# Two-layer graph network on one core: pairs of adjacency columns as one f16 stationary element, and node blocks interleaved by four

## The reference

```
def L0(X, adj, W, b):                       # W is 128x64
    deg = clip(sum(adj, 1) + 1, 1)
    h_neigh = (adj @ X + X) / deg
    out = relu(concat([X, h_neigh], 1) @ W + b)
    return out / max(norm(out), 1e-12)
def L1(F, adj, W):                          # W is 64x128
    neigh = adj @ F / (sum(adj, 1) + 1)
    return concat([F, neigh], -1) @ W.T
x = layernorm(x + L0(x, adj, W0, b0))
x = layernorm(x + L1(x, adj, W1))
```

## Time and profile before

| | us |
|---|---|
| runs, median of 3 (lowest, highest) | 773.65 (772.61, 775.78) |
| the profiled execution's own time | 773.52 |
| its span | 771.7 |
| PE busy / weight loads busy | 671.0 / 621.8 |
| DVE busy | 690.4 |
| ACT busy | 611.3 |
| POOL busy | 297.1 |
| adjacency and other transfers | 274.8 MB, 356 GB/s over the span |

### The profile page before, as it was taken

The page is one execution under the profiler, slowest core; times in us unless marked ns, Lnnn a source line. Parts: engine busy times, 40 slices in busy tenths (PEclk is TensorE's granted clock), DMA queues, the critical chain, the costliest instruction groups (busy, mean ns, idle before and its releaser), DMA issues.

```text
span 771.7 us, 31938 instructions
## 1 busy us (share of the span) xinstructions
PE 671.0 (87%) x13173; PEld 621.8 (81%) x13173; DVE 690.4 (89%) x2662; ACT 611.3 (79%) x815; POOL 297.1 (39%) x302
## 2 busy tenths in 40 slices
PE   1457787978789888999999999999999999998994
PEld 0346677868688787888899999999999999998994
DVE  4699988989999999999899999899998989888884
ACT  4879898999999898989898988787878979750032
POOL 2235523533233323365534525253444425231034
PEclk9978897989999999999999999999999999999997
DMA  9999999999999999999999999999999999900004
GB/s 301 385 420 420 417 417 420 420 419 419 420 417 420 399 419 407 412 417 405 418 407 419 407 419 401 390 375 403 386 406 379 395 384 383 393 5 3 3 18 99
DMA packets 46139, 274.79 MB, mean 356 GB/s; under 512 B 12646, under 2 KB 12710, under 8 KB 13222
## 3 DMA queue, kind: packets, MB, share of 16 engines
q1 hardware_dynamic: 45184, 270.55, 87.2%
q0 software_dynamic: 576, 2.10, 0.8%
q10 hardware_dynamic: 230, 0.07, 0.0%
HBM read 270.60 MB, written 2.10 MB: 353 GB/s over the span
## 4 chain that ended last, share of the span: by engine, by line
PE 48%; DVE 18%; issue 11%; DMA 11%; ACT 8%; POOL 3%; ACTq 0%; DVEq 0%; SPq 0%; POOLq 0%
PE s_ps L372 26%; PE u_ps L391 8%; DMA a_in<-in_adj 8%; PE p_ps L358 6%; ACT junk L570 6%; DVE t_sb L783 4%; DVE e L776 4%; DMA xl<-in_x 3%; PE z_ps L438 2%; POOL small L1158 2%; PE p_ps L450 1%; PE z_ps L423 1%; DVE a_in L783 1%; DVE q_sb L848 1%; DVE y_sb L842 1%
## 5 line engine op out<-in xcount | busy, mean ns | idle before, releaser
L570 ACT ACTIVATE junk<-a_in 128x2048 uint8<-128x2048 uint16 x256 | 489.7, 1920 | 3.8 <-DMA a_in<-in_adj 3.7
L372 PE MATMUL s_ps<-xh,t_sb 128*128 128x129 f16 x4096 | 381.8, 248 | 21.6 <-DVE t_sb L783 19.0
L372 PEld LDWEIGHTS s_ps<-xh,t_sb 128*128 128x128 fp8e4 x4096 | 308.0, 101 | 50.2 <-DVE t_sb L783 22.7
L776 DVE TENSOR_SCALAR e<-a_in 128x2048 fp8e4<-128x2048 f32 x256 | 310.9, 1223 | 11.1 <-DMA a_in<-in_adj 10.4
L1166 POOL COPY store<-pk 128x32 uint32<-128x32 uint32 (+1 forms) x250 | 215.0, 901 | 229.7 <-ACT pk L579 229.7
L358 PE MATMUL p_ps<-pow_bf,e 128*128 128x16 bf16 x4096 | 142.0, 170 | 54.1 <-DVE e L776 49.6
L358 PEld LDWEIGHTS p_ps<-pow_bf,e 128*128 128x128 fp8e4 x4096 | 128.7, 97 | 67.2 <-DVE e L776 60.1
L783 DVE TENSOR_SCALAR t_sb<-pk 128x128 uint32<-128x128 uint32 x1024 | 151.2, 221 | 6.7 <-ACT pk L579 5.6
L1158 POOL TENSOR_TENSOR small<-small,minus_half 128x4 f32<-128x4 f32 x32 | 67.8, 2117 | 199.7 <-DVE small L836 149.1
L391 PE MATMUL u_ps<-xh,u_sb 128*128 128x64 f16 x2976 | 105.0, 192 | 0.0
L391 PEld LDWEIGHTS u_ps<-xh,u_sb 128*128 128x128 fp8e4 x2976 | 99.8, 97 | 1.2
(11 more groups left out here) (119 smaller groups left out, 463.0 us busy)
## 6 DMA issues: line engine op xcount, KB each, us to landing
a_in<-in_adj SPq DMA_DIRECT2D x256, 1024.0 KB, 10.6
xl<-in_x POOLq DMA_DIRECT2D x4, 512.0 KB, 15.8
out_h<-e SPq DMA_DIRECT2D x8, 256.0 KB, 2.7
b_sb<-in_L_gnn_b ACTq DMA_DIRECT2D x3, 0.2 KB
w_sb<-in_L_gnn_W ACTq DMA_DIRECT2D x1, 32.0 KB
w_raw<-in_L_gnn_W ACTq DMA_DIRECT2D x1, 32.0 KB
```

The costliest lines, as they stand in the source:

```text
L372: last = nc.tensor.matmul(s_ps[:, n % 2, at:GW], t_sb[:, b, :], xh[:, b, at:GW], start=(b == 0), stop=False)
L570: nc.scalar.activation(junk[:, t % 2, :], halves[t % R], ACT.Copy, scale=1.0 / 128, accum_out=half_sum[:, n, c:c + 1]).then_inc(s_half, 1)
L776: nc.vector.tensor_scalar(e8[:, c, :], a_in[:, t % R, :], 1.0, None, ALU.is_equal, saturate=False).then_inc(s_e, 1)
```

## The change

Nodes are renumbered inside the kernel: four row blocks take 512 nodes, and block 4j + r holds the nodes 512j + 4p + r for p = 0 to 127. A transfer of `adj` therefore takes every fourth row, in runs of 8 KB as before. Four neighbouring columns now belong to four column blocks. The code of an entry is a byte, 60 or 61, and two neighbouring bytes read as one f16 are (1084 + a + 256 b) / 1024, with a and b the two entries. One product packs both blocks: 32 packing products per row block, each with a stationary operand of 128 f16 that lie 4 bytes apart. ACT subtracts the constant part and writes 16-bit results (256 per half). After unpacking, the two blocks of a pair are interleaved byte by byte, so every stationary operand of the sums, the catch-up and the tail has a step of 2 bytes. x and the output move in runs of 1 KB, x by ACT's queue in place of POOL's. x and `acc` no longer lie side by side; a tile `cat_in` takes the copy of x that POOL makes (`own_rows`) and the mean.

```diff
+IL = 4
+CODE = 60
+CODE_SUM = 255.0 * (1024 + CODE)
-        e8 = sb("e8", [P, NC, CH], FP8)
+        e8 = sb("e8", [P, NC, CH], U8)
-        t_sb = sb("t_sb", [P, NB, P], FP8)
+        t_sb = sb("t_sb", [P, NB // 2, 2 * P], FP8)
-        u_sb = sb("u_sb", [P, PIECE * W, P], FP8)
+        u_sb = sb("u_sb", [P, PIECE * W // 2, 2 * P], FP8)
-        xl = sb("xl", [P, NB, 2 * F], F32)
+        xl = sb("xl", [P, 2, NB, F], F32)
+        cat_in = sb("cat_in", [P, BR, 2 * F], F32)
-        x_in = xl[:, :, 0:F]
-        acc = xl[:, :, F:2 * F]
+        x_in, acc = xl[:, 0, :, :], xl[:, 1, :, :]
+        e_pair = e8[:, :, :].rearrange("p c i -> p (c i)").bitcast(F16).rearrange(
+            "p (c j i h) -> p c j i h", c=NC, i=P, h=IL // 2)
+        out_j = out.rearrange("(j p r) f -> p j (r f)", p=P, r=IL)
+        x_j = x.rearrange("(j p r) f -> p j (r f)", p=P, r=IL)
+        adj_j = adj.rearrange("(j p r) c -> j r p c", p=P, r=IL)
...
-                    sp.dma_start(a_in[:, t % R, :], adj_v[n, :, c * CH:(c + 1) * CH]).then_inc(s_in[t % R], 16)
+                    sp.dma_start(a_in[:, t % R, :], adj_j[n // IL, n % IL, :, c * CH:(c + 1) * CH]).then_inc(s_in[t % R], 16)
...
-                for b in range(CB):
-                    at = ((c % 2) * CB + b) * PK
-                    last = nc.tensor.matmul(p_ps[:, c // 2, at:at + PK], e8[:, c, b * P:(b + 1) * P],
-                                            pow_bf[:, :], start=True, stop=True)
+                for u in range(CB // 2):
+                    at = ((c % 2) * CB // 2 + u) * PK
+                    last = nc.tensor.matmul(p_ps[:, c // 2, at:at + PK], e_pair[:, c, u // 2, :, u % 2],
+                                            pow_h[:, :], start=True, stop=True)
...
-                    last = nc.tensor.matmul(s_ps[:, n % 2, at:GW], t_sb[:, b, :], xh[:, b, at:GW],
+                    last = nc.tensor.matmul(s_ps[:, n % 2, at:GW], t_sb[:, b // 2, b % 2::2], xh[:, b, at:GW],
...
-                            last = nc.tensor.matmul(u_rows[:, r, 0:F], u_sb[:, r * W + b, :],
+                            last = nc.tensor.matmul(u_rows[:, r, 0:F], u_sb[:, (r * W + b) // 2, b % 2::2],
...
+                pe.wait_ge(s_own, e + 1)
...
-                    last = nc.tensor.transpose(c_ps[:, k, :], xl[:, e * BR + k, :], ident[:, :])
+                    last = nc.tensor.transpose(c_ps[:, k, :], cat_in[:, k, :], ident[:, :])
...
+            for q in range(NC):
+                act.dma_start(x_in[:, q * CB:(q + 1) * CB, :].rearrange("p (j r) f -> p j (r f)", r=IL),
+                              x_j[:, q * CB // IL:(q + 1) * CB // IL, :]).then_inc(s_x[q], 16)
...
-                nc.scalar.copy(pk[:, n % 2, h * 512:(h + 1) * 512], p_ps[:, h, :]).then_inc(s_pk, 1)
+                nc.scalar.activation(pk_u[:, n % 2, h * 256:(h + 1) * 256], p_ps[:, h, 0:256], ACT.Copy,
+                                     bias=-CODE_SUM, scale=1024.0).then_inc(s_pk, 1)
...
-                nc.vector.tensor_scalar(e8[:, c, :], a_in[:, t % R, :], 1.0, None, ALU.is_equal,
-                                        saturate=False).then_inc(s_e, 1)
+                nc.vector.tensor_scalar(e8[:, c, :], a_in[:, t % R, :], 1.0, float(CODE), ALU.is_equal,
+                                        ALU.add).then_inc(s_e, 1)
...
-                nc.vector.tensor_tensor(acc[:, rows, :], s_sb[:, :, :], bc(small[:, 0, :], BR),
+                if e:
+                    dve.wait_ge(s_catps, e)
+                nc.vector.tensor_tensor(cat_in[:, :, F:2 * F], s_sb[:, :, :], bc(small[:, 0, :], BR),
                                         ALU.mult).then_inc(s_mean, 1)
...
-            for q in range(NC):
-                pool.dma_start(x_in[:, q * CB:(q + 1) * CB, :], x_v[:, q * CB:(q + 1) * CB, :]).then_inc(s_x[q], 16)
+            def own_rows(e):
+
+                if e:
+                    pool.wait_ge(s_catps, e)
+                else:
+                    for q in range(NC):
+                        pool.wait_ge(s_x[q], 16)
+                nc.gpsimd.tensor_copy(cat_in[:, :, 0:F], x_in[:, e * BR:(e + 1) * BR, :]).then_inc(s_own, 1)
...
                 if n:
                     keep(n - 1)
+                if e >= 0 and k == 0:
+                    own_rows(e)
```

More of the change, by code:

```diff
@@ L154, in gnn_kernel @@
         pow_f = sb("pow_f", [P, PK], F32)
-        pow_bf = sb("pow_bf", [P, PK], BF16)
+        pow_h = sb("pow_h", [P, PK], F16)
         ones_f = sb("ones_f", [P, P], F32)
@@ L213, in gnn_kernel @@
         s_mean = sem("s_mean")
+        s_own = sem("s_own")
         s_catps = sem("s_catps")
@@ L240, in gnn_kernel @@
         s_pool = sem("s_pool")
-        out_g = out.rearrange("(g k p) f -> g p k f", k=TG, p=P)
+        out_j = out.rearrange("(j p r) f -> p j (r f)", p=P, r=IL)
+        x_j = x.rearrange("(j p r) f -> p j (r f)", p=P, r=IL)
+        adj_j = adj.rearrange("(j p r) c -> j r p c", p=P, r=IL)
         out_v = out.rearrange("(e k p) f -> e p k f", k=BR, p=P)
@@ L247, in words @@
         def words(ap):
-            return ap.rearrange("p b i -> p (b i)").bitcast(U32).rearrange("p (b w) -> p b w", w=P // 4)
+            return ap.rearrange("p u i -> p (u i)").bitcast(U32).rearrange("p (u w) -> p u w", w=P // 2)
         pk_w = pk[:, :, :].rearrange("p s i -> p (s i)").bitcast(U32).rearrange("p (s w) -> p s w", s=2)
@@ L327, in _ @@
                     sp.wait_ge(s_o_dve, g - NA + 1)
-                sp.dma_start(out_g[g, :, :, :], o_sb[:, g % 4, :, :]).then_inc(s_out[g % 4], 16)
+                sp.dma_start(out_j[:, g * TG // IL:(g + 1) * TG // IL, :],
+                             o_sb[:, g % 4, :, :].rearrange("p (j r) f -> p j (r f)", r=IL)).then_inc(s_out[g % 4], 16)
             for i in range(4):
@@ L449, in tail_sums @@
                         if j < NV:
-                            last = nc.tensor.matmul(v_ps[j % 3][:, r, :], v_sb[:, j % VR, r * W + b, :],
+                            last = nc.tensor.matmul(v_ps[j % 3][:, r, :], v_sb[:, j % VR, (r * W + b) // 2, b % 2::2],
                                                     xh[:, at + b, 0:HP], start=(b == 0), stop=(b == W - 1))
@@ L453, in tail_sums @@
                         for part in range(2):
-                            last = nc.tensor.matmul(v_ps[j % 3][:, r, 0:F], v_sb[:, j % VR, r * W + b, :],
+                            last = nc.tensor.matmul(v_ps[j % 3][:, r, 0:F], v_sb[:, j % VR, (r * W + b) // 2, b % 2::2],
                                                     xh[:, at + b, part * F:(part + 1) * F],
@@ L718, in _ @@
             nc.vector.tensor_scalar(id8[:, :], ident[:, :], 2.0, None, ALU.mult, saturate=False)
-            nc.vector.tensor_copy(pow_bf[:, :], pow_f[:, :]).then_inc(s_pow, 1)
+            nc.vector.tensor_copy(pow_h[:, :], pow_f[:, :]).then_inc(s_pow, 1)
             link(nc.vector.memset(xh[:, :, 2 * HP:GW], XS))
@@ L790, in unpack @@
                     dve.wait_ge(s_sum, (n - 1) * 2 + h + 1)
-                half = slice(h * NB // 2, (h + 1) * NB // 2)
+                half = slice(h * NB // 4, (h + 1) * NB // 4)
                 dst = words(t_sb[:, half, :])
-                unpack_planes(lambda g: dst[:, :, g * PKW:(g + 1) * PKW],
-                              pk_w[:, n % 2, :].rearrange("p (b w) -> p b w", w=PKW)[:, half, :]).then_inc(s_t, 1)
+                unpack_planes(lambda g: dst[:, :, g * 2 * PKW:(g + 1) * 2 * PKW],
+                              pk_w[:, n % 2, :].rearrange("p (u w) -> p u w", w=2 * PKW)[:, half, :]).then_inc(s_t, 1)
             def unpack_piece(n):
@@ L801, in unpack_piece @@
                     dve.wait_ge(s_ups, turn(n))
-                dst = words(u_sb[:, 0:(r1 - r0) * W, :])
-                unpack_planes(lambda g: dst[:, :, g * PKW:(g + 1) * PKW],
-                              stored(q - 1, r0, r1 - r0).rearrange("p (b w) -> p b w", w=PKW)).then_inc(s_u, 1)
+                dst = words(u_sb[:, 0:(r1 - r0) * W // 2, :])
+                unpack_planes(lambda g: dst[:, :, g * 2 * PKW:(g + 1) * 2 * PKW],
+                              stored(q - 1, r0, r1 - r0).rearrange("p (u w) -> p u w", w=2 * PKW)).then_inc(s_u, 1)
             def add_piece(n):
@@ L895, in unpack_tail @@
                     dve.wait_ge(s_vps, j - VR + 1)
-                dst = v_sb[:, j % VR, :, :].rearrange("p b i -> p (b i)").bitcast(U32).rearrange(
-                    "p (r b w) -> p r b w", r=TG, w=P // 4)
-                src = stored(NQ - 1, g * TG, TG).rearrange("p (r b w) -> p r b w", r=TG, w=PKW)
-                unpack_planes(lambda t: dst[:, :, :, t * PKW:(t + 1) * PKW],
-                              src[:, :, i * W:(i + 1) * W, :]).then_inc(s_v, 1)
+                dst = v_sb[:, j % VR, :, :].rearrange("p u i -> p (u i)").bitcast(U32).rearrange(
+                    "p (k u w) -> p k u w", k=TG, w=P // 2)
+                src = stored(NQ - 1, g * TG, TG).rearrange("p (k u w) -> p k u w", k=TG, w=2 * PKW)
+                unpack_planes(lambda t: dst[:, :, :, 2 * t * PKW:2 * (t + 1) * PKW],
```

(2 more changed lines are left out.)

3 lines of the change are left out of this document (2 added, 1 removed).

## The result

The changed kernel takes 763.65 us (median of 4 runs, 763.23 to 764.5), the kernel before 773.79 beside it. The ratio is 0.9871, 95% interval 0.986 to 0.9883: faster by 10.1 us, or 1.3%. The forecast was 758.5 us, 15.2 us faster, in a range of 749 to 773.

The account below looks back on a forecast made before the run. Transfers bound 30 to 200 us, PE 500 to 675 us, with a mixed stage between. Gains 7.8 + 2.5 + 1.0 + 3.5 + 0.4 = 15.2 us off 773.5 gave a forecast of 758.5 us, range 749 to 773.

Parts of the forecast that it names:

- Packing at the f16 load's price: Packing, 64 to 32 products per row block: f16 products assumed 24.4 ns apart as now, so 0.78 us per row block goes.
- rival 1: Packing: the f16 load costs two fp8 loads (49 ns), PE keeps its late pace; 769.6 us, chance 0.22.
- Strided fp8 operands at no cost: Sums, catch-up and tail: fp8 columns 2 bytes apart were taken to cost nothing.
- rival 2: Catch-up and tail: strided fp8 loads take about 50 ns and the kernel gets slower, 826 us; chance 0.14.
- Late 7.8: 500 to 675 us, 16.2 row blocks: pace from 10.78 to 10.3 us, gain 7.8 us, bounds 0 and 12.5.
- middle 2.5: 200 to 500 us, 29.4 row blocks: 2.5 us from halved packing, bounds 0 and 5.6, the time over the floor.
- drain (after the last transfer) 1.0: 675 to 690 us, PE busy throughout: 40 of 80 packing products go, 1.0 us, bounds 0 and 1.0.
- The floor of 10.01 us: Transfers' limit per row block: 4.194 MB at 419 GB/s take 10.01 us.
- The late pace of 10.3 us: 500 to 675 us: DVE is next to bind, 9.93 us of work plus 0.37 of waits per row block.
- x and its queue: 5 to 30 us: 3.5 us gained, bounds 0 and 4.5; ACT's four issues cost 1.5 us, over before its first sum.
- Output: End of the kernel, output in 1 KB runs: 0.4 us gained, bounds 0 and 0.7.
- rival 3: PE's clock: idling more, PE is granted 1.2 GHz longer, eating 2.5 + 3.9 us; about 765 us, chance 0.08.

Follow-up runs that it names:

- pack_twice: The changed kernel with each packing product issued twice, 64 per row block again, same result: 774.05 us, ratio 1.0006.
- one_plane: The changed kernel with seven of eight planes of DVE's catch-up unpacking left out from row block 36 on (wrong results): 762.85 us, ratio 0.9868.
- both_less: The changed kernel, from row block 36 on, without seven of eight planes of DVE's catch-up unpacking and half of PE's catch-up products: 761.2 us, ratio 0.983.
- x_pool: The changed kernel with x issued by POOL again, still in 1 KB runs: 758.95 us, ratio 0.9812.
- x_sp: The changed kernel with x's four transfers issued by SP, each behind one of the first four chunks, 1 KB runs: 758.58 us, ratio 0.9811.
- before_x_act: The kernel before with x issued by ACT's queue in place of POOL's, still in 256 B runs: 780.53 us, ratio 1.0091.
- act_more: The changed kernel with a second conversion of 256 columns on ACT beside each one: 764.35 us, ratio 0.988.

## Why the prediction was right or wrong

- **Packing at the f16 load's price: right.** 0.39 us for 16 products (`pack_twice`), 24.4 ns each, as assumed; rival 1 (49 ns) is out. Of the two statements quoted from the Trainium skill (TensorE: Matmul & The Clock Gate, "Weight-path perf modes") the one on chunks and column counts describes this kernel, the one on two bf16 at a time doesn't.
- **Strided fp8 operands at no cost: right**, 1.80 and 1.44 us as before; rival 2 is out.
- **The stream's gain: right in sum by luck, wrong in place.** Late 7.8, middle 2.5 and drain (after the last transfer) 1.0 make 11.3 us. From row block 12 to the last compare the two kernels differ by 0.7 + 10.6 = 11.3, and `pack_twice` gives packing 10.4. But the middle's 2.5 us, drawn from packing's 5.5% of that chain, is no gain of packing: `pack_twice` has the same 327.4 us there. The floor of 10.01 us came from 30 to 200 us; in 200 to 500 us the kernel before itself has its chunks land 2.57 us apart, 10.28 us a row block, so the stage stood at its floor and the 5.6 us over it weren't there to win. I had also spread an average of 300 us over row blocks of two kinds: up to row block 44 fewer products bring nothing, behind it lies the late pace with all of the loss.
- **The late pace of 10.3 us: right, for a wrong reason.** Measured are 4.194 / 0.409 = 10.25 us. The step said that DVE's 9.93 us plus waits set it. With 1 us of DVE's work gone the pace stayed (`one_plane`), and with PE's relief beside it too (`both_less`). The transfers set it, at 10.3 us; that DVE's sum gave the same number is luck.
- **x and its queue: the step that failed.** It gave 3.5 us to the 1 KB runs, and these are worth 3.5 to 4, with the output's. It then costed ACT's four issues at the 0.37 us of an issue of the output, 1.5 us, "long over when the first chunk is summed". They took 12.85 us, because the last of them took 11.0 us, and everything of ACT behind it waited too. Charged are 4.7 to 5.1 us (`x_pool`, `x_sp`). In place of the 3.5 us won stand 2.0 lost by row block 12, 5.5 us off; the forecast was 5.1 us too low. The price came from an issue of the output, 1024 runs of 256 B on a queue with next to nothing in it. A transfer of x has 512 runs, fewer than that, and the first three of them took 0.40 to 0.78 us. So the number of runs in one transfer is not what the step missed; it is what stands in the queue already. In `before_x_act`, with 2048 runs in a transfer, the first issue took 0.40 us and the second 12.5. POOL's own issues of x, 1.15 us each, stood in the same trace and delayed no engine that had early work.
- **Output: not contradicted**, 0.4 assumed; an output lands after 2.2 in place of 2.7 us, and the last part of the kernel, which holds some of the drain's gain as well, is 0.8 us shorter. No run changed the output alone.
- **Clock (rival 3):** it fell, 0.82 in place of 0.88 in 30 to 200 us, and cost nothing that can be measured. With as few products `x_pool` has 0.83 there and `x_sp` 0.88, so part of the difference is scatter between profiles.
- **`own_rows`, the compare, `take_packed`, the row distance in `adj`: as costed.** POOL's copy takes 396 ns, below its lower bound; the compare 1222 ns; the conversion 377 ns. `x_pool` moves 418 to 420 GB/s from 30 to 200 us with every fourth row.

## What to carry to other kernels

A transfer's issue is work of the engine that issues it: behind other transfers of hundreds of runs in its queue it held ACT for 11.0 and 12.5 us here, so an engine that has early work of its own should not issue a bulk load ahead of it. Put such loads on an engine that has nothing to do yet or among those of the queue that streams anyway, in the order in which they are needed. When a saving is counted in a stage, count it by the units of work (row blocks) that the stage holds, and ask whether the engine that is relieved holds any of them. Take the floor that the transfers set from the same stage, by the distance of their landings: here it was 10.3 us and not the 10.0 of an earlier stage, and four experiments looked for an engine that held what the transfers held.

## What the runs showed of the hardware that was not expected

- An issue can hold its engine for long: 11.0 us for one of 512 runs of 1 KB (12.85 for the four), 19.8 us for four of 2048 runs of 256 B each, both on ACT. The first of the four took 0.40 us both times; with 512 runs each the fourth was held, with 2048 the second (12.5 us). On SP the same four issues of 1 KB runs took 0.42 to 0.69 us each when they alternated with chunks, with one chunk's issue at 2.85 us.
- Packing products whose stationary operand is 128 columns of f16, 4 bytes apart, follow each other as fast as with 128 neighbouring fp8: 16 in 0.39 us.
- 2.1 MB in 256 B runs among the stream cost 3.7 us more than in 1 KB runs (344 against 405 GB/s in 5 to 30 us).
- PE's granted clock in the early row blocks was lower with fewer products (0.76 against 0.87 in 60 to 100 us; 0.79 to 0.84 in `x_sp`, `x_pool` and `act_more`) without a loss of time that can be measured.
- Saturated 1 MB transfers land 2.48 us apart, but about one in eleven after 3.4 us, in every kernel of this record between 200 and 500 us: 10.2 to 10.3 us for four in place of 9.9.
